# Mamba's decays in three pairs of buffers, the third in SBUF in the context's place, and VectorE's product with C made once over both units of a pair

## The reference, cut to what matters

```python
dt = softplus(einsum('bsr,er->bse', dt, dtp_w) + dtp_b)
dA = exp(dt[..., None] * A)                          # the decays
dBu = dt[..., None] * Bm[:, :, None, :] * xi[..., None]
def step(h, t):
    da, dbu, c = t
    h = da * h + dbu                                 # the scan over time
    return (h, einsum('bes,bs->be', h, c))           # the product with C, summed over the states
...
y = (ys + xi * Dp) * silu(z)
```

## Time and profile before

| what | us |
|---|---|
| median of 3 runs | 6634.21 |
| the profiled execution | 6639.8 |
| its span, first to last instruction | 6638.0 |
| VectorE busy | 4928.1 (74%) |
| GpSimd busy | 4394.1 (66%) |
| ScalarE busy | 3620.5 (55%) |
| TensorE busy (matmul) | 6129.0 (92%) |

### The profile page before, as it was taken

One profiled execution on the slowest core, in us unless ns is written; L12 is line 12 of the kernel. 1 busy time (PEld: TensorE's weight loads), 2 busy tenths in 40 slices (PEclk: granted clock), 3 DMA queues, 4 the chain that ended last, 5 costly groups with the idle time before them and its releaser, 6 DMA issues. The chain is left out here.

```text
span 6638.0 us, 60681 instructions
## 1 busy us (share of the span) xinstructions
PE 6129.0 (92%) x20586; PEld 2577.4 (39%) x20586; DVE 4928.1 (74%) x5709; ACT 3620.5 (55%) x6605; POOL 4394.1 (66%) x2056
## 2 busy tenths in 40 slices
PE   9999999999999989898899989898989898988898
PEld 4555555544443333323333323333323343323444
DVE  4444445543225999999999999999999999995623
ACT  4444445432225666666666666666666666664432
POOL 3333334323005999999999999999999999992300
PEclk9999999999998989899989999999999898989998
DMA  2000000213002333333333333332333232332000
GB/s 80 1 1 1 1 1 1 86 26 102 20 0 68 83 76 78 78 93 85 72 89 71 83 88 86 71 89 65 89 81 93 65 89 65 93 80 56 4 0 26
DMA packets 228678, 387.64 MB, mean 58 GB/s; under 512 B 46304, under 2 KB 64416, under 8 KB 225936
## 3 DMA queue, kind: packets, MB, share of 16 engines
q1 hardware_dynamic: 228368, 383.75, 23.7%
HBM read 207.14 MB, written 23.40 MB: 35 GB/s over the span
## 5 line engine op out<-in xcount | busy, mean ns | idle before, releaser
L2506 POOL TENSOR_TENSOR work<-work,weights 128x1024 f32<-128x1024 f32 x1152 | 2685.6, 2361 | 15.8 <-PE banks L2384 6.8
L2429 DVE TENSOR_TENSOR_SCAN banks<-banks,work 128x512 f32<-128x512 f32 x1584 | 1985.7, 1272 | 53.5 <-ACT banks L2474 48.1
L2384 PE MATMUL banks<-work 128*64 128x512 f32 x4608 | 1353.9, 670 | 378.2 <-POOL work L2511 271.1
L2474 ACT ACTIVATE banks<-work 128x512 f32<-128x512 f32 x2304 | 1496.0, 680 | 25.5
L1992 PE MATMUL banks<-work,weights 128*128 128x512 f32 (+31 forms) x3796 | 1140.6, 451 | 3.0 <-DVE work L2222 3.0
L2237 DVE TENSOR_TENSOR work<-banks,weights 128x512 f32<-128x512 f32 x1584 | 1056.0, 668 | 0.0
L2511 POOL TENSOR_TENSOR work<-work,weights 128x1024 f32<-128x1024 f32 x360 | 848.0, 2356 | 238.4 <-ACT work L2129 238.4
L2429 DVE TENSOR_TENSOR_SCAN work<-banks,work 128x512 f32<-128x512 f32 x720 | 911.2, 1269 | 99.8 <-ACT banks L2474 97.2
L603 POOL TENSOR_TENSOR work<-work 128x1024 f32<-128x1024 f32 x256 | 479.6, 1893 | 743.4 <-DVE work L470 742.9
L1992 PEld LDWEIGHTS banks<-work,weights 128*128 128x128 f32 x3796 | 634.4, 190 | 600.0 <-issue 523.6
L2133 ACT ACTIVATE work<-banks 128x2 f32<-128x2 f32 x792 | 135.9, 172 | 1227.4 <-DVE work L2237 1225.6
(11 more groups left out here) (312 smaller groups left out, 6796.9 us busy)
## 6 DMA issues: line engine op xcount, KB each, us to landing
weights<-mamba_bc SPq DMA_DIRECT2D x592, 256.0 KB, 5.0
work<-work SPq DMA_DIRECT2D x1160, 128.0 KB, 2.3
weights<-mamba_taps SPq DMA_DIRECT2D x5, 2048.0 KB, 7.5
weights<-cross_vo SPq DMA_DIRECT2D x16, 512.0 KB, 6.9
mamba_taps<-work SPq DMA_DIRECT2D x4, 2048.0 KB, 7.8
cross_vo<-weights SPq DMA_DIRECT2D x6, 1024.0 KB, 8.4
work<-in_conv_rows SPq DMA_DIRECT2D x16, 256.0 KB, 6.7
out_T<-X SPq DMA_DIRECT2D x8, 512.0 KB, 3.3
```

Source lines behind the costliest of these rows:

```text
L2384: mm = e.matmul(ybank[k % 2][64 * h:64 * h + 64, :], fold, ring_pair(n, j)[:, h, :], start=False, stop=(a == SP_ - 1))
L2429: e.tensor_tensor_scan(ub if by_pool(j) else da, da, ub, state[:, i:i + 1], ALU.mult, ALU.add).then_inc(scanned, 1)
L2474: e.activation(banks[:, slot_of(i), :], dt_rep[:, k % 2, h, :], ACT.Exp, scale=decay[:, f:f + 1]).then_inc(da_full, 1)
L2506: e.tensor_tensor(ring_pair(n, j), u_rep[:, k % 2], bc[:, a, 0, :].unsqueeze(1).to_broadcast([P, 2, TC]), ALU.mult) \
```

## The change

1. The decays get three pairs of buffers in turn: banks 0 and 1, banks 2 and 3, and `core.C` in SBUF. `decay_slots` gives each of the 36 x 32 = 1152 pairs the slot that was used longest ago; in the last step only the two in PSUM are used. ScalarE's wait before the decays of a pair is therefore on the pair three before, not two before, in all steps but the last. The state copies (`keep_state`) are made at that same place, for every pair up to the one whose slot is taken.
2. `times_c` is one instruction of 128x1024 over both units of a pair, and stands behind the scan of the next pair's first unit. In a pair whose decays lie in `core.C`, both scans and the product read two SBUF tensors.
3. In the last step SyncE loads the context again into `core.C` with three DMAs (`reload_context`), after the wait for the step before, and the stage's end waits for them.

```diff
+def decay_slots():
+    slot, earlier, last = [], [], [None, None, None]
+    for g in range(STEPS * PAIRS_N):
+        slots = range(3) if g < (STEPS - 1) * PAIRS_N else range(2)
+        s = min(slots, key=lambda t: -1 if last[t] is None else last[t])
+        slot.append(s)
+        earlier.append(last[s])
+        last[s] = g
+    return slot, earlier
...
-    slot_of = lambda i: 2 * (i // 2 % 2) + i % 2
+    slot, earlier = decay_slots()
+    decays = [banks[:, 0:2, :], banks[:, 2:4, :], core.C[:]]
+    pair_at = lambda N, j: val(N, PAIRS_N, j)
+    decay_pair = lambda N, j: decays[slot[pair_at(N, j)]]
+    step_of = lambda g: (0, g // PAIRS_N)
+    last_in_c = max(g for g in range(STEPS * PAIRS_N) if slot[g] == 2)
...
+    def keep_state(e, g):
+        M, j = step_of(g), g % PAIRS_N
+        if by_pool(j):
+            e.wait_ge(scanned, scanned_at(M, 2 * j + 1))
+            e.activation(state[:, 2 * j:2 * j + 2], ring_pair(M[1], j)[:, :, TC - 1], ACT.Copy).then_inc(kept, 1)
+        else:
             e.wait_ge(prod_d, prod_d_at(M, j))
-            e.activation(state[:, 2 * j:2 * j + 2], banks[:, s:s + 2, TC - 1], ACT.Copy).then_inc(saved, 1)
+            e.activation(state[:, 2 * j:2 * j + 2], decay_pair(M, j)[:, :, TC - 1], ACT.Copy).then_inc(saved, 1)
+
+    def slots_free(e, N, j):
+        g = earlier[pair_at(N, j)]
+        if g is None:
+            return
+        before = earlier[pair_at(N, j) - 1]
+        for m in range(0 if before is None else before + 1, g + 1):
+            keep_state(e, m)
+        M, j = step_of(g), g % PAIRS_N
+        if not by_pool(j):
             e.wait_ge(saved, saved_at(M, j))
...
-    def times_c(e, N, n, j, h):
-        i = 2 * j + h
-        last = e.tensor_tensor(ring_pair(n, j)[:, h, :], banks[:, slot_of(i), :], bc[:, j % SP_, 1, :], ALU.mult)
-        if h == 1:
-            last.then_inc(prod_d, 1)
+    def times_c(e, N, n, j):
+        e.wait_ge(scanned, scanned_at(N, 2 * j + 1))
+        e.tensor_tensor(ring_pair(n, j), decay_pair(N, j), bc[:, j % SP_, 1, :].unsqueeze(1).to_broadcast([P, 2, TC]), ALU.mult) \
+            .then_inc(prod_d, 1)
...
+    def reload_context(e):
+        M, j = step_of(last_in_c), last_in_c % PAIRS_N
+        e.wait_ge(saved, saved_at(M, j)) if not by_pool(j) else e.wait_ge(scanned, scanned_at(M, 2 * j + 1))
+        e.dma_start(core.C[:, 0, :], core.dram["ctxT"][0:P]).then_inc(context_back, 16)
+        for r in (0, DC - P):
+            e.dma_start(core.C[r:r + DC - P, 1, :], core.dram["ctxT"][P:DC]).then_inc(context_back, 16)
...
                         if h == 0 and j > 0 and not by_pool(j - 1):
-                            e.wait_ge(scanned, scanned_at(N, i - 1))
-                            times_c(e, N, n, j - 1, 1)
-                        if h == 1 and not by_pool(j):
-                            e.wait_ge(scanned, scanned_at(N, i - 1))
-                            times_c(e, N, n, j, 0)
+                            times_c(e, N, n, j - 1)
```

More of the change, by code:

```diff
@@ L1953, in mamba @@
     da_full, fed, scanned, prod_d, prod_q, summed = S("da_full"), S("fed"), S("scanned"), S("prod_d"), S("prod_q"), S("summed")
-    gated = S("gated")
+    gated, context_back = S("gated"), S("context_back")
     y_full, y_free, y_added = S("y_full"), S("y_free"), S("y_added")
@@ L1964, in mamba @@
     prod_d_at = lambda N, j: val(N, ND, d_index(j) + 3)
-    saved_at = lambda N, j: val(N, ND, d_index(j) + 3)
+    saved_at = lambda N, j: val(N, ND, d_index(j) + 1)
     prod_q_at = lambda N, j: val(N, NQ, q_index(j) + 1)
@@ L2121, in soft_plus @@
         e.activation(dt[:, tv, :], lane_v, ACT.Softplus, bias=lv("dt_b", tv)).then_inc(ln.v_free, 1)
[L2123 to L2127, removed]
+    def keep_state(e, g):
+        M, j = step_of(g), g % PAIRS_N
+        if by_pool(j):
             e.wait_ge(scanned, scanned_at(M, 2 * j + 1))
-            e.activation(state[:, 2 * j:2 * j + 2], ring_pair(m, j)[:, :, TC - 1], ACT.Copy).then_inc(kept, 1)
-        elif N[1] >= 0:
-            s = slot_of(2 * j)
+            e.activation(state[:, 2 * j:2 * j + 2], ring_pair(M[1], j)[:, :, TC - 1], ACT.Copy).then_inc(kept, 1)
+        else:
             e.wait_ge(prod_d, prod_d_at(M, j))
-            e.activation(state[:, 2 * j:2 * j + 2], banks[:, s:s + 2, TC - 1], ACT.Copy).then_inc(saved, 1)
+            e.activation(state[:, 2 * j:2 * j + 2], decay_pair(M, j)[:, :, TC - 1], ACT.Copy).then_inc(saved, 1)
[8 more added lines that the diff above has]
+        if not by_pool(j):
             e.wait_ge(saved, saved_at(M, j))
@@ L2307, in _ @@
                     spread_u(e, 1)
+                    if pair_at(N, 0) == (STEPS - 1) * PAIRS_N:
+                        reload_context(e)
                     if c == CHUNKS - 1:
@@ L2339, in _ @@
             e.wait_ge(rep_in[1], 128 * 2 * STEPS)
+            e.wait_ge(context_back, 48)
             e.wait_ge(core.first_loaded, FIRST_LOAD * (LAYERS + 1))
@@ L2427, in _ @@
                         e.wait_ge(da_full, da_full_at(N, i))
-                        da, ub = banks[:, slot_of(i), :], ring_pair(n, j)[:, h, :]
+                        da, ub = decay_pair(N, j)[:, h, :], ring_pair(n, j)[:, h, :]
                         e.tensor_tensor_scan(ub if by_pool(j) else da, da, ub, state[:, i:i + 1], ALU.mult, ALU.add).then_inc(scanned, 1)
                         if h == 0 and j > 0 and not by_pool(j - 1):
-                            e.wait_ge(scanned, scanned_at(N, i - 1))
-                            times_c(e, N, n, j - 1, 1)
-                        if h == 1 and not by_pool(j):
-                            e.wait_ge(scanned, scanned_at(N, i - 1))
-                            times_c(e, N, n, j, 0)
+                            times_c(e, N, n, j - 1)
                         if h == 1 and j == PAIRS_N - 1 and not by_pool(j):
-                            e.wait_ge(scanned, scanned_at(N, i))
-                            times_c(e, N, n, j, 1)
+                            times_c(e, N, n, j)
             N = (LAYERS // 2, 0)
@@ L2471, in _ @@
                         if h == 0:
-                            slots_free(e, N, n, j)
+                            slots_free(e, N, j)
                         f = (2 * k + h) * SP_ + a
-                        e.activation(banks[:, slot_of(i), :], dt_rep[:, k % 2, h, :], ACT.Exp, scale=decay[:, f:f + 1]).then_inc(da_full, 1)
+                        e.activation(decay_pair(N, j)[:, h, :], dt_rep[:, k % 2, h, :], ACT.Exp, scale=decay[:, f:f + 1]).then_inc(da_full, 1)
                         if c == CHUNKS - 1 and i == H_OUT[0]:
```

## The result

The changed kernel takes 7604.7 us (median of 4 runs, 7600.89 to 7610.48) where the kernel before takes 6635.4 beside it: a ratio of 1.146, 95% interval 1.1443 to 1.1477. The forecast was 7650, with a range of 7400 to 8000. The profiled execution took 7605.3 us against 6639.8 before: +965.5 us, where the prediction's sum was +1007.

A forecast was written before the change was run, and what follows sets the result against it. VectorE was taken to set the pace, with GpSimd 3.3 us a step behind. The profiled 6639.8 us, +1109 for exclusion, -47 for merging and -55 for the third pair gave 7647, stated as 7650; range 7400 to 8000.

The forecast's parts named there:

- Where the third pair lies: VectorE's scans and products on `core.C` and GpSimd's reading instructions exclude each other in turn: +1109 us over 373 pairs.
- C0: First scan of a pair in `core.C`: meets GpSimd at any point of its beat, waits 1.07 us.
- C1: Second scan of that pair: waits 1.04 us with a product between, 2.16 without, 1.39 together.
- GpSimd's own loss: GpSimd's instructions held out by VectorE's in turn: 2.73 us a pair in `core.C`, 1020 us.
- The merged product, -47: VectorE's one product of 128x1024 for two of 128x512: 0.06 us saved for each of 792 pairs.
- The third pair, -55: ScalarE running three pairs ahead removes half of VectorE's 111 us of waiting for decays in the steady part.
- its lower bound: The third pair's least gain: none, as waits for GpSimd's fed pairs replace VectorE's waits for decays.
- The rest, "nothing": ScalarE's decay writes to SBUF, later state copies and SyncE's context reload were each counted as adding no time.
- No exclusion: Rival: VectorE reads both SBUF operands beside GpSimd without waiting, so the change is faster, 6510 us; 5%.
- products only: Rival: VectorE's products with two SBUF inputs exclude GpSimd but its scans don't; 6800 us; 4%.
- TensorE's clock: Rival: TensorE's granted clock falls and TensorE becomes the bound; 8585 us at 1.2 GHz throughout; 5%.
- The 65 us: Saving estimated from lower fixed cost of SBUF than PSUM for 1002 VectorE instructions in `core.C`; counted as nothing.

The follow-up runs named there:

- e3: Against the kernel before: merged products, decays of only GpSimd's ten pairs a step in `core.C`, so scans but no products have two SBUF inputs; 7457.9 us, ratio 1.1232.
- e6: The changed kernel with GpSimd's products on the ring replaced by two memsets each, so it writes and hardly reads; scans run on zeros; 6886.1 us.
- e2: The changed kernel with three buffer pairs kept but two products of 128x512 a pair in place of the merged one; 7951.1 us, ratio 1.1982.
- e1: The kernel before with the merged product alone: two buffer pairs in PSUM, nothing in `core.C`, no reload; 6663.9 us, ratio 1.004.
- e12: The changed kernel with products apart (two a pair) and GpSimd's work on the ring as memsets; 6869.0 us, ratio 1.035.
- e7: The kernel before with GpSimd's products on the ring replaced by two memsets each; scans run on zeros; 6615.0 us, ratio 0.9966.
- e10: The changed kernel with GpSimd's ring work as memsets and ScalarE's pieces between the decays one pair later; 6527.4 us, ratio 0.9834.
- e11: The changed kernel with ScalarE's pieces between the decays one pair later and nothing left out; 7507.4 us, ratio 1.1311.

## Why the prediction was right, point by point

**Where the third pair lies: right, and by its mechanism.** Scans with two SBUF inputs exclude as products do (e3), by GpSimd's reads alone (e6 against the changed kernel), by whole instructions and in turn (the collision at 4020.96, e2). The sum's term of 1109 us measured 1017. A scan waited 1.06 us where the working gives (1.07 + 1.39)/2 x 0.95 = 1.17, a product 0.88 where it gives 0.92. The scans of the trace, told apart by their place in the pair, show which step is off. C0 waited 1.12 us in the mean, not 1.07 x 0.95 = 1.02: 37 us too little in the sum. C1 waited 1.01, not 1.39 x 0.95 = 1.32: 115 us too much. With a product between it waited 0.85 (255 pairs), and directly behind C0 1.37 (118 pairs), where the working has nearly a whole instruction of GpSimd each time; three in ten of those 118 waited less than 0.1 us. One reason is that GpSimd is there less often: it is busy 91% of the steady part (4244 of 4662 us), and I took 95%. Whether that is all of it stays open. GpSimd's own loss, 1020 us in the prediction, measured 767: 1152 x 0.481 + 360 x 0.372 + 74 x 0.426 (the form of L2277, 2788 ns for 2362) + 74 x 0.636 (L2280).

The page "SBUF — State Buffer" of the Trainium skill, section "Who interferes with whom", says that a VectorE instruction with two SBUF inputs contends with a GpSimd instruction that reads SBUF, and not with one that only writes it. The traces agree, for scans too: beside GpSimd's products a scan from `C` lasts 2.26 to 2.49 us, beside memsets 1.27 to 1.30 (e6).

**The merged product, -47: the spacing right, the conclusion wrong.** VectorE's busy time fell by 46.5 us in e1, and the kernel took 26.5 us more. The prediction asked when TensorE gets the pair, and whether VectorE itself has to wait, but not when ScalarE gets the pair's buffers back. That wait grew by 69 us, more than the product saves.

**The third pair, -55: wrong in sign.** I saw ScalarE's 1219.9 us of waiting as room and half of VectorE's 111 us as a gain. VectorE's waits for decays did fall, from 111 to 42 us in the steady part, but its waits for GpSimd's fed pairs rose from 3 to 85, which is what the prediction named for its lower bound; in all its idle time before scans rose from 153 to 160 us. With the collisions out of the way the third pair costs 254 us (e12 against e7), and with ScalarE's pieces moved a pair later the change wins 88 us (e10 against e7), inside the -47 to -158 that the prediction gave it without exclusion; some 55 us of collisions with `times_x` are still in e10.

**The rest, "nothing": the step that failed.** I went through ScalarE's state copies and SyncE's reload, and not through the other pieces in ScalarE's queue that wait for TensorE. Their places (L2126, L2127, L2162 of the new kernel) were written for an engine two pairs ahead. Moving them gives back 97 us (e11). The two errors, one of 92 us too much for the collisions and one of 62 us too little for VectorE's idle time (-55 taken, +7 measured), partly cancelled. So the nearness of the forecast, 45 us, is in part luck: single terms missed by more.

**The rivals.** No exclusion and products only: fallen by e3 and the changed kernel's own groups. TensorE's clock did fall, from 0.941 to 0.895 in the mean and to 0.84 in a step, and a sum of the ring takes 725 ns for 670; two thirds of a step at the lower of the two levels would be a granted clock of about 0.67, and VectorE's idle time before scans is put down to GpSimd and ScalarE, not to TensorE. The 65 us that the Trainium skill's page "VectorE: DVE Perf Modes", section on the TRN2 errata, would have given for reading SBUF did not show either: in e6, beside memsets, the median scan from `C` lasts 1259 or 1271 ns and the median scan from `banks` 1268 or 1271.

## What to carry to other kernels

Before an operand of VectorE is moved from PSUM to SBUF beside a busy GpSimd, count the inputs: with two in SBUF, each instruction here waited 0.9 to 1.2 us in the mean, somewhat under half of GpSimd's instruction of 2.36 us, and GpSimd lost three quarters as much (767 against 1017 us). A buffer more lets an engine run ahead, and every piece in its queue whose place was fitted to the old distance may have to move with it; look for once-a-step waits of several us in the waits of the engine that got the room. Merging two instructions on a full engine saves what their starts lie apart beyond the merged one (here 0.06 us of 1.18), but moves the moment at which the first half's buffer comes free: read who waits for it.

## What the runs showed of the hardware that was not expected

An instruction of GpSimd on two columns (L2280) lasts 833 ns in the mean in place of 197 when VectorE's instructions with two SBUF inputs run beside it: it waits 0.64 us in the mean, and the large ones 0.37 to 0.48. Memsets of GpSimd, 951 ns for 128x1024, did not lengthen VectorE's instructions with two SBUF inputs (medians of e6) and were not lengthened by them (951 ns in both e6 and e7). Cutting a merged product in two made each half wait longer than the whole (1.25 against 0.88 us in the mean). In e2 the first halves, which stand directly behind the pair's second scan, wait 1.56 us, and the second halves, one free scan later, 0.93. ScalarE's Exp to SBUF takes 712 ns where the same to PSUM takes 680.
